# An ODE scan with a mixture-of-experts network behind it: the matmuls whose results nobody reads are left out

## What is computed

```python
def _derivative(q, p, drive, coupling, bias):
    dq = q - q ** 3 / 3.0 - p + drive + tanh(q) @ coupling.T + bias
    dp = EPSILON * (q + ALPHA - BETA * p)
    return (dq, dp)
# _rk4_step: four derivatives a step (Runge-Kutta), then clip; drive = x[:, t]
# over all 128 steps: q_trace (16, 128, 256)
probs = softmax(q_trace @ W_router.T); rw, sel = top_k(probs, 2)
sh = (silu(x @ Wg) * (x @ Wu)) @ Ws_down * sigmoid(x @ W_sgate.T)     # shared, 704 wide
eo = (silu(gate_e) * up_e) @ We_down[e]                               # 8 experts, 176 wide
out = input + sh + sum_e combine[t, e] * eo
```

## Time and profile before

| | |
|---|---|
| time, median of 3 runs | 676.11 us (675.38 to 677.73) |
| the profiled execution: its time | 675.66 us |
| its span, first to last instruction | 673.8 us |
| what lies around the span | 1.9 us |
| PE (TensorE matmul) busy | 640.3 us, 95% |
| DVE (VectorE) busy | 616.9 us, 92% |
| ACT (ScalarE) busy | 402.1 us, 60% |
| POOL (GpSimd) busy | 181.5 us, 27% |
| mean granted clock of TensorE | 0.972 of full speed |

### The profile page before, as it was taken

How to read it: one execution, slowest core, us unless ns; L and a number is a source line. 1 busy time by engine, 2 the same in 40 slices (tenths; PEclk the granted TensorE clock), 3 DMA queues, 4 the chain that set the end, 5 groups by cost and what they waited for, 6 DMA issues and landing times.

```text
span 673.8 us, 33901 instructions
## 1 busy us (share of the span) xinstructions
PE 640.3 (95%) x12832; PEld 608.7 (90%) x12832; DVE 616.9 (92%) x4190; ACT 402.1 (60%) x2244; POOL 181.5 (27%) x404
## 2 busy tenths in 40 slices
PE   3688999999999999999999999999999999999998
PEld 2578899999999999999999999999999999999997
DVE  6799999999999999989999899999999999999961
ACT  2866565656566565656656565665656665665653
POOL 0001123232322323232232323223232322323243
PEclk9975899999999999989999899999999999999999
DMA  8800000000000000000000000000000000000000
GB/s 302 259 2 2 3 3 3 12 3 12 2 12 4 3 12 3 11 3 12 3 3 11 2 12 3 12 3 3 12 2 12 3 12 4 3 11 3 12 2 17
DMA packets 8627, 13.65 MB, mean 20 GB/s; under 512 B 1520, under 2 KB 7984, under 8 KB 8208
## 3 DMA queue, kind: packets, MB, share of 16 engines
q1 hardware_dynamic: 8464, 11.50, 5.0%
HBM read 9.40 MB, written 2.10 MB: 17 GB/s over the span
## 4 chain that ended last, share of the span: by engine, by line
DVE 67%; PE 21%; issue 7%; ACT 3%; DMA 0%; POOL 0%; DVEq 0%; SPq 0%; POOLq 0%
DVE th_lo L741 10%; DVE hidden L822 9%; DVE force L759 8%; DVE cubic L744 7%; PE up_ps L563 6%; DVE p_sum L713 6%; PE down_ps L578 6%; DVE q L766 5%; DVE y L713 5%; DVE rest L713 3%; DVE q_raw L766 3%; PE coup_ps L511 3%; PE coup_ps L505 3%; DVE x_rest L662 2%; DVE w L701 2%
## 5 line engine op out<-in xcount | busy, mean ns | idle before, releaser
L563 PE MATMUL up_ps<-q_hi,w 128*128 128x128 f16 x2176 | 240.2, 221 | 0.2 <-POOL q_lo L869 0.2
L901 POOL TENSOR_TENSOR hidden<-hidden,comb_s 128x128 f32<-128x128 f32 x272 | 123.2, 455 | 330.0 <-DVE force L759 257.6
L389 ACT ACTIVATE th_hi<-q 128x32 f16<-128x32 f32 x384 | 88.0, 229 | 196.3 <-DVE q L766 194.2
L563 PE MATMUL up_ps<-q_lo,w 128*128 128x128 f16 x1088 | 203.2, 222 | 0.0
L505 PE MATMUL coup_ps<-th_hi,c 128*128 128x16 f16 x4096 | 181.5, 171 | 1.9 <-ACT th_hi L389 1.8
L578 PE MATMUL down_ps<-hidden,wd 128*128 128x128 f32 x1088 | 180.3, 289 | 0.0
L563 PEld LDWEIGHTS up_ps<-q_hi,w 128*128 128x128 f16 x2176 | 178.5, 99 | 0.4 <-POOL q_lo L869 0.4
L505 PEld LDWEIGHTS coup_ps<-th_hi,c 128*128 128x128 f16 x4096 | 139.7, 97 | 6.7 <-ACT th_hi L389 2.6
L578 PEld LDWEIGHTS down_ps<-hidden,wd 128*128 128x128 f32 x1088 | 142.0, 191 | 0.0
L511 PE MATMUL coup_ps<-th_lo,c 128*128 128x16 f16 x2048 | 131.0, 172 | 7.3 <-DVE th_lo L741 4.6
L511 PEld LDWEIGHTS coup_ps<-th_lo,c 128*128 128x128 f16 x2048 | 86.3, 97 | 25.6 <-DVE th_lo L741 11.5
(11 more groups left out here) (95 smaller groups left out, 1094.1 us busy)
## 6 DMA issues: line engine op xcount, KB each, us to landing
wf<-in_w_up SPq DMA_DIRECT2D x1, 4224.0 KB, 12.9
wd<-in_w_down SPq DMA_DIRECT2D x1, 2048.0 KB, 22.7
out<-out_s SPq DMA_DIRECT2D x16, 128.0 KB, 2.2
xs<-in_x SPq DMA_DIRECT2D x1, 1920.0 KB, 19.1
sel<-in_spread SPq DMA_DIRECT2D x1, 408.0 KB, 18.8
cf<-in_coupling SPq DMA_DIRECT2D x1, 256.0 KB, 2.5
xs<-in_x SPq DMA_DIRECT2D x1, 128.0 KB, 2.5
ident<-in_identity SPq DMA_DIRECT2D x1, 64.0 KB, 2.4
```

What stands on the lines that cost most here:

```text
L563: last = nc.tensor.matmul(up_ps[(f * TILES + j) % UPS][:, h * TOK:(h + 1) * TOK], w16[:, part, k, h, j * P:(j + 1) * P], q[:, k, :], start ...
L901: nc.gpsimd.tensor_tensor(hidden[:, j, :], hidden[:, j, :], comb_s[:, j, :], ALU.mult).then_inc(weighed, 1)
```

## The change

Both kinds of unread matmul go, with the table that sizes the first kind. No other instruction, wait or order is touched.

```diff
-def units(st):
-
-    halves = sum(u.count(st) for u in UP_AT)
-    downs = DOWN_AT.count(st) + DOWN_AT.count(st + STAGES) + (st == 0)
-    return 6 * halves + 8 * downs + 4 * SPREAD_AT.count(st)
-
-
-WARM = [min(6, max(0, 11 - units(st))) for st in range(STAGES)]
...
-                if n > STAGES:
-                    for _ in range(WARM[st - 1]):
-                        nc.tensor.matmul(coup_ps[:, 2 * P:3 * P], c16[:, 0, 0, 0:P], c16[:, 0, 0, 0:P],
-                                         start=False, stop=True, skip_group_check=True)
-
                 pe.wait_ge(hi_ready, n + 1)
...
-                    if b == 0 and st >= STAGES // 2:
-
-                        for _ in range(8):
-                            nc.tensor.matmul(up_ps[0][:, 0:P], c16[:, 0, 0, 0:P], c16[:, 0, 0, 0:P], start=True,
-                                             stop=True)
```

## The result

| | before | after |
|---|---|---|
| median | 675.75 us (4 runs, 674.57 to 677.73) | 689.73 us (4 runs, 688.72 to 689.93) |
| ratio | | 1.0201 (95%: 1.0174 to 1.0228) |
| profiled execution: time, span | 675.66, 673.8 us | 688.72, 686.9 us |
| falls of the clock at the 14 block boundaries from the third block on | 2, one stretch each | 14, ten of them two stretches long |
| L766 / L748 waits for `coup_ps` | 3.4 us, 11 times | 16.5 us, 43 times |

I forecast slower, 681.5 us in a range of 678.0 to 687.5. The direction and the mechanism hold; the size is more than twice the forecast and outside the range.

What follows compares the result with a forecast made beforehand. The prediction took DVE to set the pace, with TensorE fitting in only at full clock. Ten falls of 0.75 us, less 1.9 us already paid and 0.2 us, gave +5.4 us: 681.5 us, range 678.0 to 687.5.

Steps and rivals of the forecast that it cites:

- What bounds the kernel: All stages: DVE sets a pace of 1.20 us a stage, and TensorE fits in only at full clock.
- L498 on the path, -0.2 us: Stage 3's six unread matmuls: up to 0.02 us on the path in 15 blocks, taken as -0.2 us.
- L596, 0: First block's second half: its 128 unread matmuls are covered by DVE's preparation of weights, so removing them changes 0.
- The number of falls: Block boundaries from block 2 on: clock falls at 10 of 14, where two fell before; bounds 2 and 14.
- The cost of a fall: Each clock fall at a block boundary: 0.75 us, of which 0.05 for falls longer than one stretch.
- The argument about the early fall: A fall starting a stage or two earlier spends part of itself on stage 2, saving about one excess of 0.48 us.
- Rival B: Block boundaries: all 14 fall, some for two stretches; +11.2 us, 687.3 us, or 692 us with second stretches; chance 0.17.
- Rival A: Whole kernel: no further falls, since the clock falls only where TensorE waits long for work; 675.5 us; chance 0.09.
- Rival C: TensorE's queue: unread matmuls delay the th_hi matmuls at half clock, so removal is faster; 673.1 us; chance 0.03.
- Falls at stages 5 and 8: Sign of being wrong: falls at other thin places, holding only a down tile, whose neighbours lose three unread matmuls each.

Runs made afterwards that it cites:

- e9: Kernel before; first block's unread matmuls now eleven in each of stages 22-31, second block filled to eleven a stage, later blocks eight more in stage 2: 671.68 us.
- e10: e9 without the six unread matmuls ahead of stage 3's th_hi matmuls, and with ten instead of eight behind stage 2's coupling matmuls: 671.58 us.
- e2: Kernel before without the first block's 128 unread matmuls (L596); the 312 of L498 stay: 675.56 us, ratio 0.9986.
- e3: Kernel before with the 312 unread matmuls of L498 streaming 32 columns instead of 128, same number and place: 679.05 us, ratio 1.0034.
- e11: Kernel before with at most one unread 128-column matmul where L498 had three or six: 679.46 us, ratio 1.0065.
- e1: Kernel before without the 312 unread matmuls of L498; the first block's 128 (L596) stay: 689.85 us, ratio 1.0196.
- e4: Kernel before with the same 21 unread matmuls a block moved from the thin stages to stages holding network work: 690.43 us, ratio 1.0207.
- e12: Changed kernel plus eight unread matmuls behind the coupling matmuls of stage 2 in each block from the third on: 683.10 us, ratio 1.0108.
- e6: Kernel before with only the 15 unread matmuls of stages 0 to 3 in each block; stages 6 and 9 and L596 lose theirs: 676.12 us.

## Why the prediction was right or wrong

- **What bounds the kernel: right.** The waits of the closing instruction for the coupling went from 11 to 43 (30 to 40 were forecast). Undisturbed stages keep their 1.21 us with and without unread matmuls, and the undisturbed blocks of e9 are before's 38.8.
- **L498 on the path, -0.2 us: right within 0.1 us.** e10 against e9 puts stage 3's six at 0.1 us in the whole.
- **L596, 0: right.** e2 is before within its interval, and the first block's logits are copied at 58.3 in before and after.
- **The number of falls: wrong, and the first half of the miss.** The step took 10, "nearer to all than to none", since "a fall lengthens its block and moves all that follows". There were 14. In e3 and e11 the next boundary is spared behind each fall. Without any unread matmul none is, although the falls begin anywhere from 0.04 us ahead of the logits' copy to 2.51 us behind it: I read this as a thin run wide enough that no shift of 0.8 to 1.2 us gets past it.
- **The cost of a fall: wrong, the larger half.** I took 0.75 us and put only 0.05 in it for falls of two stretches. Ten of the 14 were of two. By the block lengths they cost 40.0 - 38.8 = 1.2 us, and the four short ones 39.6 - 38.8 = 0.8. The argument about the early fall was right in its first step (it spends its first part on stages it can't lengthen: the two stages of 1.21 us shown above) and wrong in its conclusion, that this makes it cheap. All ten falls that began in stage 1 or 2 lasted two stretches, and all four that began in stage 3 lasted one. e1 and e4 have the same line: long up to 1.91 us behind the copy, short from 2.02. An early fall still has thin stages in its first stretch, goes on for a second, and the second lies on the full stages. With stage 2 filled (e12), seven of the nine falls that began in stages 1 and 2 were short. The sum with these sizes: 10 x 1.2 + 4 x 0.8 - 2 x 0.95 = +13.3 us, and the second block 42.8 against 43.6 = -0.8: +12.5, against 13.1 of span. With the copies read to 0.01 us from the timelines it closes: 12.4 for the ten, 3.3 for the four, 1.9 less for before's two and 0.7 less for the second block, +13.1.
- **Rival B was what happened**, in both its parts (falls at all boundaries, and a second stretch in some). It had 0.17. Its first figure, 687.3 us, counted short falls at 0.95 each; the measured 689.7 lies between that and its longer case, 692.
- **Rival A** is out with the 14 falls, and so is the rule on idle gaps of the Trainium skill ("TensorE: Matmul & The Clock Gate", "Why this matters for your kernels") as the only cause: TensorE was busy 3.38 of the 3.42 us ahead of the fall at 342.09 (last section), and 3.04 of 3.41 ahead of before's at 298.48. **Rival C** looks as if it had one true grain, the second block's 0.8 us, but e12 has the same code as the changed kernel up to there and took 43.7 us for it (58.2 to 101.9). So this is luck in where the clock rose and fell, not the queue, and not a gain of the change; without it the miss would have been some 0.8 us larger.
- **Named in the prediction as what would make it wrong** was a fall above 0.95 us; that came. Falls at stages 5 and 8 didn't, also in e6, which takes just those unread matmuls away. The falls were to begin in stages 2 to 4 of most blocks: ten began in stages 2 and 3, four in stage 1.

What stays open: why a given boundary of before falls in one execution and not in the next. All runs fit an observation by the chip that drifts against the blocks, but none was made to move it. That it runs free of the kernel is what the Trainium skill says ("TensorE: Matmul & The Clock Gate", Part 1). How e3 and e11 come to the same was not taken further than the two sizes.

## What to carry to other kernels

Matmuls that nobody reads may be what keeps TensorE at full clock; before they are removed, find the stages where TensorE has least to do, since it is there alone that they worked here (e4, e6), and price a fall by the full stages that stand behind the thin ones. Where a fall may start inside a thin run, count two stretches, not one. When filling thin stages, keep each stage's TensorE work below the pace of the engine that sets it, and put the filling behind the instructions on the path: here that turned a kernel with two late falls in its profile into one with none, 0.5% faster and steady to 0.4 us.

## What the runs showed of the hardware that I had not expected

- Falls of the clock came with TensorE busy for nearly the whole stretch ahead: 3.38 of 3.42 us in the changed kernel, and the clock fell at 342.09. Of the 57 matmuls in it 45 are coupling matmuls of 16 or 32 columns.

```profile
338.67:342.09 3.42, 3.38 (x57) 2.99 (x57) 3.11 (x23) 1.95 (x11) 0.80 (x2) 1.00 0.02 5
```

  A 16-column matmul counts 0.17 us of busy time each in the profile (L492), though eight of them in a row take 0.36 us from the first's start to the last's end:

```profile
339.83 0.36 PE L492 MATMUL coup_ps<-th_hi,c 128*128 128x16 f16 x8
```

  So the busy share says little about how many columns pass.
- The clock that a page grants before the first clock event of a trace isn't a reading. In the changed kernel the first event is at 65.6 us, the page shows 9 until there, and the stages from 61.84 to 65.20 take the 1.68 us of half clock. So e1 shows a mean clock of 0.918 and the changed kernel 0.938 with the same falls; only means over stretches after the first event compare.
